# Two attention layers and two FFNs on one core: another order of the preparations in the first units, a wider spacing of stages in the FFN, other PSUM banks at its end and in the tail

## What is computed

```python
x = x + L0_xattn(ln(x), ctx)     # 32 query heads, 8 key/value heads of 128, rotary embedding, mask per batch
x = x + L0_ffn(ln(x))            # 512 -> 2 x 1376, silu(gate) * up, -> 512; weights are 4-bit with scale and zero per group
x = x + L1_xattn(ln(x), ctx)     # the same sizes, rms norm of q and k in place of rotary, one mask
x = x + L1_ffn(ln(x))            # router over 128 slots, top 8, softmax, gate from an uncertainty score; adds to ln(x)
```

## Time and profile before

| | PE | DVE | ACT | POOL |
|---|---|---|---|---|
| busy, us of 2639.3 | 2511.0 | 1813.5 | 1179.0 | 1063.3 |
| share | 95% | 69% | 45% | 40% |
| busy in 50 to 92 us | 27.77 | 37.37 | 25.19 | 21.48 |
| busy in 92 to 177 us | 67.77 | 57.02 | 41.39 | 38.38 |

### The profile page before, as it was taken

One profiled execution on the slowest core, in us unless ns is written; L12 is line 12 of the kernel. 1 busy time (PEld: TensorE's weight loads), 2 busy tenths in 40 slices (PEclk: granted clock), 3 DMA queues, 4 the chain that ended last, 5 costly groups with the idle time before them and its releaser, 6 DMA issues. The chain is left out here.

```text
span 2639.3 us, 45860 instructions
## 1 busy us (share of the span) xinstructions
PE 2511.0 (95%) x18307; PEld 1391.1 (53%) x18339; DVE 1813.5 (69%) x3271; ACT 1179.0 (45%) x2281; POOL 1063.3 (40%) x844
## 2 busy tenths in 40 slices
PE   7789999999999999999999889999999999999997
PEld 3355555555555554443444456665655655555543
DVE  7687887878777888643444556677776767765665
ACT  4555454545454544322222354444444444544333
POOL 3445444555544555222221243333334333334332
PEclk8899999999999999999999989999999999999999
DMA  6000000101000000101100100001010101000001
GB/s 193 17 25 17 33 25 25 33 9 33 9 33 17 12 7 25 41 25 32 34 16 15 36 17 1 1 33 40 10 33 9 33 9 33 25 15 1 1 1 64
DMA packets 57254, 68.73 MB, mean 26 GB/s; under 512 B 9858, under 2 KB 32966, under 8 KB 57040
## 3 DMA queue, kind: packets, MB, share of 16 engines
q1 hardware_dynamic: 57044, 65.79, 7.9%
HBM read 61.59 MB, written 4.19 MB: 25 GB/s over the span
## 5 line engine op out<-in xcount | busy, mean ns | idle before, releaser
L729 PE MATMUL PB<-WB,AR 128*128 128x512 f16 x3072 | 700.4, 382 | 25.8 <-issue 9.8
L685 PE MATMUL PB<-XTB,WB 128*128 128x512 f16 x3072 | 690.9, 383 | 3.4 <-DVE XTB L1634 3.4
L685 PEld LDWEIGHTS PB<-XTB,WB 128*128 128x128 f16 x3072 | 300.6, 99 | 352.9 <-issue 17.7
L729 PEld LDWEIGHTS PB<-WB,AR 128*128 128x128 f16 x3072 | 295.5, 98 | 359.3 <-issue 29.7
L1798 DVE SCALAR_TENSOR_TENSOR X<-PB,SML,X 128x512 f32<-128x512 f32 x256 | 191.6, 750 | 207.6 <-PE PB L729 201.1
L2312 POOL TENSOR_TENSOR AR<-AR,SML 128x512 f32<-128x512 f32 x128 | 144.7, 1152 | 327.1 <-DVE SML L1768 327.1
L1264 ACT ACTIVATE AR<-PB 128x512 f16<-128x512 f32 x256 | 132.2, 600 | 233.8 <-PE PB L768 233.8
L845 PE MATMUL PB<-XTB,AR 128*128 128x512 f16 (+1 forms) x864 | 199.5, 389 | 0.0
L1702 DVE TENSOR_TENSOR AR<-PB,AR 128x512 f16<-128x512 f32 x128 | 87.7, 688 | 159.4 <-ACT AR L1234 159.0
L2306 POOL TENSOR_TENSOR AR<-AR 128x512 f32<-128x512 f32 x128 | 185.8, 1451 | 24.5 <-DVE AR L1668 16.0
L2332 POOL TENSOR_TENSOR SML<-SML 128x16 f32<-128x16 f32 x32 | 98.1, 3065 | 239.3 <-DVE SML L1710 239.3
(11 more groups left out here) (222 smaller groups left out, 4010.6 us busy)
## 6 DMA issues: line engine op xcount, KB each, us to landing
STG<-in_wo SPq DMA_DIRECT2D x14, 1024.0 KB
STG<-in_wq SPq DMA_DIRECT2D x13, 1024.0 KB
STG<-in_qw_gu SPq DMA_DIRECT2D x40, 128.0 KB
STG<-in_ctxT SPq DMA_DIRECT2D x4, 1024.0 KB
X<-in_x SPq DMA_DIRECT2D x4, 1024.0 KB, 10.8
out_x<-X SPq DMA_DIRECT2D x16, 256.0 KB, 2.4
STG<-in_wk SPq DMA_DIRECT2D x14, 256.0 KB
STG<-in_wv SPq DMA_DIRECT2D x14, 256.0 KB
```

The costliest lines, as they stand in the source:

```text
L685: m = pe.do.matmul(b[:, :], wq[x][:, k, h * 128:(h + 1) * 128], XT[y][c][:, k, :], start=n == 0, stop=n == 11)
L729: m = pe.do.matmul(b[:, :], AT[x][:, h, t * 128:(t + 1) * 128], wo[y][:, h, :], start=n == 0, stop=n == 11)
```

## The change

No arithmetic is changed but the way that one low half is made. Five parts:

1. **First three units.** `w(0, 0, 2)` leaves `BY_POOL`: DVE makes its low half, and ACT's second pass and POOL's four subtractions are gone. The layer norm of chunk 1 comes earlier in unit 0: turned behind queries 2 and 3 in place of behind query 3 and between two empty output slots. In unit 2 the `scale` of context chunk 2 moves from slot 1 to slot 2. Ahead of the units, `w(0, 1, 1)` is prepared earlier, the mask and `w(0, 1, 0)` later.
2. **FFN.** For the three weights of layer 1's first head, `amax`, `peak`, `scale` and the two `low` move from slots (c=2, 2), (2, 3), (3, 0), (3, 2), (3, 3) of their slice to (2, 3), (3, 1), (3, 2), (3, 3) and slot 0 of the next slice. `peak` and `scale` of `w(1, 1, 0)` move one slot on.
3. **Last slice.** `down` uses banks 6, 7, 2, 3 for its four tiles.
4. **Start of layer 1.** Keys and values of unit 1 run ahead of the scores of unit 0, around `turn_k(0)`. Chunk 1's layer norm comes later in unit 0, and `w(1, 1, 2)` gets its `peak` in slot 8 and the rest in unit 1.
5. **Tail.** The normalised tiles of chunks 0 and 1 are turned one slot later, in banks 2, 3, 1, 6; `t_q` moves from slot 7 to slot 8; `TB_LG` and `TB_W` use bank 6 in place of 2.

```diff
-        BY_POOL = {("w", 0, 0, 2), ("w", 1, 0, 0), ("w", 1, 0, 1), ("w", 1, 0, 2), ("w", 1, 1, 0), ("w", 1, 1, 1), ("w", 1, 1, 2)}
+        BY_POOL = {("w", 1, 0, 0), ("w", 1, 0, 1), ("w", 1, 0, 2), ("w", 1, 1, 0), ("w", 1, 1, 1), ("w", 1, 1, 2)}
...
+        for slot, *stage in ((1, "ln_stats"), (2, "ln_norm", 0), (3, "ln_turn", 0), (3, "ln_norm", 1), (4, "ln_low", 0),
+                             (4, "ln_turn", 1), (5, "ln_low", 1)):
+            plan(0, 0, slot, stage[0], 0, 1, *stage[1:])
         plan_at(0, ("c", 1), (0, 0), (0, 1, 2), (0, 2, 3), (0, 3), (0, 4))
-        plan(0, 0, 1, "ln_stats", 0, 1)
-        plan_ln(0, 0, 0, 1, False)
...
-        plan_at(0, ("c", 2), (1, 9), (2, 0, 6), (2, 1, 7), (2, 4), (2, 7))
+        plan_at(0, ("c", 2), (1, 9), (2, 0, 6), (2, 2, 7), (2, 4), (2, 7))
...
-        plan_ln(1, 0, 2, 1, False)
-        plan(1, 0, 0, "peak", w(1, 1, 2), 6)
-        plan(1, 0, 1, "scale", w(1, 1, 2), 7)
+        for slot, *stage in ((1, "ln_norm", 0), (4, "ln_turn", 0), (5, "ln_low", 0), (5, "ln_norm", 1), (7, "ln_turn", 1),
+                             (8, "ln_low", 1)):
+            plan(1, 0, slot, stage[0], 2, 1, stage[1])
+        plan(1, 0, 8, "peak", w(1, 1, 2), 3)
+        plan(1, 1, 0, "scale", w(1, 1, 2), 7)
...
-                (u - 1, 9, ("t_stats", c)), (u, 1, ("t_norm", c, 0)), (u, 2, ("t_turn", c, 0)), (u, 3, ("t_norm", c, 1)),
-                (u, 5, ("t_turn", c, 1)), (u, 7, ("t_q", c)), (u + 1, 1, ("t_up", c)), (u + 1, 1, ("t_rq", c)),
+                (u - 1, 9, ("t_stats", c)), (u, 1, ("t_norm", c, 0)), (u, 3, ("t_turn", c, 0)), (u, 4, ("t_norm", c, 1)),
+                (u, 6, ("t_turn", c, 1)), (u, 8, ("t_q", c)), (u + 1, 1, ("t_up", c)), (u + 1, 1, ("t_rq", c)),
...
-        TB_TURN = {0: (2, 3, 0, 1), 1: (2, 3, 0, 1), 2: (6, 7, 6, 7), 3: (6, 7, 1, 3)}
+        TB_TURN = {0: (2, 3, 1, 6), 1: (2, 3, 1, 6), 2: (6, 7, 6, 7), 3: (6, 7, 1, 3)}
...
-        TB_R, TB_A, TB_LG, TB_W = (2, 2, 7, 7), (3, 3, 1, 1), (2, 2, 4, 2), (2, 2, 4, 4)
+        TB_R, TB_A, TB_LG, TB_W = (2, 2, 7, 7), (3, 3, 1, 1), (6, 6, 4, 2), (6, 2, 4, 4)
...
-            plan_prep_f(w(1, 0, s - 1), (s, 2, 2), (s, 2, 3), (s, 3, 0), (s, 3, 2), (s, 3, 3))
+            plan_prep_f(w(1, 0, s - 1), (s, 2, 3), (s, 3, 1), (s, 3, 2), (s, 3, 3), (s + 1, 0, 0))
...
-        plan_prep_f(w(1, 1, 0), (5, 0, 3), (5, 1, 0), (5, 1, 1), (5, 1, 3), (5, 2, 0))
+        plan_prep_f(w(1, 1, 0), (5, 0, 3), (5, 1, 1), (5, 1, 2), (5, 1, 3), (5, 2, 0))
...
+        def down_bank(s, t):
+
+            return 6 + t % 2 if s < 5 or t < 2 else t
...
-                else:
+                elif u > 1:
                     keys_values(u, 0)
                     keys_values(u, 1)
...
             for h in range(4):
                 queries(1, 0, h)
+            keys_values(1, 0)
             turn_k(0)
+            keys_values(1, 1)
             norm_q(0)
```

More of the change, by code:

```diff
@@ L349, in plan_at @@
                 plan(L, u, slot, *stage, *bank)
+        for slot, *stage in ((1, "ln_stats"), (2, "ln_norm", 0), (3, "ln_turn", 0), (3, "ln_norm", 1), (4, "ln_low", 0),
+                             (4, "ln_turn", 1), (5, "ln_low", 1)):
+            plan(0, 0, slot, stage[0], 0, 1, *stage[1:])
         plan_at(0, ("c", 1), (0, 0), (0, 1, 2), (0, 2, 3), (0, 3), (0, 4))
-        plan(0, 0, 1, "ln_stats", 0, 1)
-        plan_ln(0, 0, 0, 1, False)
         plan_at(0, w(0, 0, 2), (0, 9), (1, 0, 6), (1, 1, 7), (1, 2), (1, 3))
+        plan_ln(0, 2, 0, 2)
+        plan_at(0, ("c", 2), (1, 9), (2, 0, 6), (2, 2, 7), (2, 4), (2, 7))
         plan_at(0, w(0, 1, 2), (1, 5), (1, 7, 6), (1, 8, 7), (2, 0), (2, 1))
-        plan_ln(0, 2, 0, 2)
-        plan_at(0, ("c", 2), (1, 9), (2, 0, 6), (2, 1, 7), (2, 4), (2, 7))
         plan_prep(0, 3, ("c", 3))
@@ L379, in build @@
             plan(0, 30, hi, "unpack_hi", 0, k)
-        plan_ln(1, 0, 2, 1, False)
-        plan(1, 0, 0, "peak", w(1, 1, 2), 6)
-        plan(1, 0, 1, "scale", w(1, 1, 2), 7)
+        for slot, *stage in ((1, "ln_norm", 0), (4, "ln_turn", 0), (5, "ln_low", 0), (5, "ln_norm", 1), (7, "ln_turn", 1),
[3 more added lines that the diff above has]
+        plan(1, 1, 0, "scale", w(1, 1, 2), 7)
         for half in range(2):
-            plan(1, 0, 2 + half, "low", w(1, 1, 2), half)
+            plan(1, 1, 1 + half, "low", w(1, 1, 2), half)
         plan_ln(1, 2, 2, 2)
@@ L857, in down @@
                 for t in t01:
-                    b = bank(6 + t % 2, (x_add, ("f", s, c, t)))
+                    b = bank(down_bank(s, t), (x_add, ("f", s, c, t)))
                     e, last = 0, 3 * len(tiles) - 1
@@ L1078, in tensor @@
             ln_turn(0, 0, 1)
+            peak(w(0, 1, 1), 4)
             keep_warm(10, 0)
+            scale(w(0, 1, 1), 4)
             queries(0, 0, 0)
-            peak(w(0, 1, 1), 4)
             peak(w(0, 1, 0), 5)
             queries(0, 0, 1)
-            scale(w(0, 1, 1), 4)
             scale(w(0, 1, 0), 5)
@@ L1281, in ln_turn @@
                     if i == 0 and c == 3:
-                        act.wait_ge(w_lop, (w(0, 0, 2), 3))
+                        act.wait_ge(w_lo, (w(0, 0, 2), 3))
                     if i > 0:
@@ L1521, in scalar @@
             high(w(0, 0, 0))
+            high(w(0, 1, 1))
             turned_q(0, 0)
             turned_q(0, 1)
-            high(w(0, 1, 1))
             turned_q(0, 2)
@@ L1528, in scalar @@
             queries_0(0, 1)
+            high(w(0, 1, 0))
             queries_0(0, 2)
-            high(w(0, 1, 0))
             queries_0(0, 3)
@@ L1908, in down @@
                     dve.wait_ge(*added[c, t])
-                    dve.do.scalar_tensor_tensor(xs, PB[6 + t % 2][:, :], CY[:, :], xs, ALU.mult, ALU.add
+                    dve.do.scalar_tensor_tensor(xs, PB[down_bank(s, t)][:, :], CY[:, :], xs, ALU.mult, ALU.add
                                                 ).then_inc(x_add.of(("f", s, c, t)), 1)
@@ L2213, in vector @@
             ln_low(0, 0, 0)
+            largest(w(0, 1, 1))
+            peak(w(0, 1, 1), 4)
             low(w(0, 0, 0), 0)
             low(w(0, 0, 0), 1)
+            scale(w(0, 1, 1), 4)
             ln_low(0, 0, 1)
             keys_0(0)
-            largest(w(0, 1, 1))
             largest(w(0, 1, 0))
-            peak(w(0, 1, 1), 4)
             peak(w(0, 1, 0), 5)
             turned_q(0, 0)
-            mask()
-            scale(w(0, 1, 1), 4)
-            scale(w(0, 1, 0), 5)
-            turned_q(0, 1)
             low(w(0, 1, 1), 0)
             low(w(0, 1, 1), 1)
+            turned_q(0, 1)
+            scale(w(0, 1, 0), 5)
+            mask()
             queries_0(0, 0)
@@ L2234, in vector @@
             low(w(0, 1, 0), 0)
+            queries_0(0, 3)
             low(w(0, 1, 0), 1)
             turned_k(1)
-            queries_0(0, 3)
             values_0(1)
```

## The result

| | before | changed kernel |
|---|---|---|
| median of the runs, us | 2646.20 (2643.47 to 2647.24) | 2616.61 (2615.51 to 2617.64) |
| profiled execution, us | 2641.13 | 2616.46 |
| its span, us | 2639.3 | 2614.7 |

The ratio is 0.989, with a 95% interval of 0.9873 to 0.9907: 29.6 us less in the median, 24.7 in the profiled executions. The two differ because the profiled execution of the kernel before, 2641.13, was faster than each of its four other runs, while the changed kernel's lies at its median. The prediction was 2613.0, range 2603 to 2630.

The account below looks back on a forecast made before the run. PE, busy 95% of the span, was taken as the bound. Terms of -14.5, -4.6, -2.4, -3.6 and -8.5 us sum to -33.6, giving a profile of 2607.5 and a median of 2613.0 us, range 2603 to 2630.

Parts of the forecast that it names:

- A, first output of unit 0: In unit 1: with the low half on DVE this output starts at 111.5 in place of 120.6; -11.5 us.
- A, unit 0: Turns of chunk 1 in unit 0 waited 6.3 us for ACT's norm; 0 gained, DVE being busy.
- A, unit 2: Unit 2: `scale` of `c2` one query further back, -6.0 us; +3 for new waits at output tiles.
- B: FFN slices 1 to 3: waits at `peak` and `scale` go, partly given back through loads; -4.6 us, bounds 0 and -7.3.
- C: Last FFN slice: a `peak` wait of 3.04 us and part of a 3.54 go; -2.4 us, bounds 0 and -5.5.
- D: Unit 0 of layer 1: `norm_q`'s 2.6 us is covered, the turn of unit 1's keys waits 5.0; -3.6 us.
- E: Tail: 9.7 us of waits covered, new ones at `weigh` and one turn; -8.5 us, bounds -6 and -10.
- DVE takes the time back: Rival, first units onward: every low half blocked and each add late on DVE; only -14, 2632.6 us; chance 0.13.
- The load chain: Rival, FFN: the low half ends 2.7 us later in slices 1 and 2; -26 in all, about 2620.5; chance 0.10.
- The first part does what it says: Rival denied this: unit 0's output waits for something else ready shortly before 120.6; -23, 2623.5 us; chance 0.07.
- Little is given back: Rival: givebacks of 3 (first units), 2.8 (FFN) and 5.0 us (layer 1's start) don't come; -42, 2604.5; chance 0.10.
- The clock in 92 to 177 us: Rival, units 1 to 3: more frequent waits keep PE's clock at 0.50; slower, 2680 us if all halved; chance 0.03.

Follow-up runs that it names:

- Experiment 1: Changed kernel with POOL making the low half of `w(0, 0, 2)` again, behind a second pass of ACT; median 2624.14 us.
- experiment 2: Changed kernel with the two low halves of `w(0, 0, 2)` one slot earlier on DVE, slots 1 and 2 of unit 1; median 2608.39 us.
- experiment 6: Changed kernel with the layer norm of chunk 1 in unit 0 planned as before the change; one time, 2615.37 us.
- experiment 12: Changed kernel with the preparations of `w(0, 1, 1)`, `w(0, 1, 0)` and the mask ahead of the units in their old order; median 2616.97 us.
- experiment 10: Changed kernel with the `scale` of context chunk 2 back in slot 1 of unit 2; one time, 2621.01 us.
- Experiment 3: Changed kernel with SP loading the 4-bit words of slices 3 and 4 ahead of the layer 1 weights that wait; median 2609.37 us.
- Experiment 5: Changed kernel with unit 1's keys and values of layer 1 behind the scores of unit 0 again; median 2617.24 us.
- experiments 7: Changed kernel with the low halves of `w(0, 1, 2)` in slots 2 and 3 of unit 2 in place of 0 and 1; one time, 2617.66 us.

## Why the prediction came out as it did

The time lay 3.6 us above the forecast and inside the range; the change of the profile was forecast as -33.6 and was -24.7. That the median came so near is in part luck: the forecast was made on the profiled execution of before, 5.1 us below the median of its runs, and the changed kernel's profile shows 9.0 us more than the 2607.5 forecast for it. By the prediction's own sign ("wrong it is if the shift by unit 4 is under 10"), its largest part was wrong: the shift there is 6.7. By its own steps:

**A, first output of unit 0: right mechanism, wrong size.** Predicted -11.5, measured -4.4 (from the scores of unit 1, 0.3 late, to those of unit 2, 4.1 early). Three terms of one sum failed. "DVE may begin when the first pass has ended, at 105.7": the pass ended at 106.04 and DVE began at 107.92, because the instruction ahead of it waited for ACT (1.9 us). "I take 5.8 us for all of it": 107.92 to 115.87 are 7.95 (2.15 us), the low halves being 6.4 of it, near the upper bound of 7.0 that the prediction itself gave. "The clock behind a short wait should not fall, -2.4": the wait was still 4.85 and the output took 10.88, not 7.93 (3.0 us). With 0.1 at the hand-over they are the 7.1 that this output missed. The clock's part is the least certain: in nine other profiles with a wait of 4.8 the output took 9.32 to 9.62, once 10.88, so it fell every time, by 1.4 to 3.0 us, and the step gained 4.4 to 5.9. Experiment 1 shows that the low half was what held the output, experiment 2 that the order on DVE held the low half: with the pair one slot earlier, wait and lower clock are both gone, which is the state that the prediction had assumed.

**A, unit 0: right in this profile.** 0 predicted, 0.3 measured; most other profiles come 2 to 4 us later, with the lower clock of the first queries, which the prediction did not consider. The 6.3 at the turns became 2.5 there and 3.5 more at `weigh`. The reason given, a busy DVE, holds in the main; experiment 6 puts the early norm at 1.5, and experiment 12 the order ahead of the units at nothing.

**A, unit 2: right in sum, wrong in its parts.** -6.0 and +3 were predicted, -2.7 measured. The 3.9 of wait in the -6.0 does not follow from the rows: a query of 2.75 further back leaves 3.2 of the 5.9, and no term covers these. The new waits are larger than the 0.7 to 0.9 assumed (0.5, 2.1 and 2.4), and experiment 10 shows that the new slot, to which the whole -6.0 was put down, gives 1.2 by itself.

**B: right**, in sum and slice by slice. The chain of low half, load and words was read rightly: 8.15 us from low half to first use, 8.1 before; new wait 2.71, forecast 2.8. Experiment 3 takes the chain away and gains 7.2. The -1.3 of slice 2 has a fall of the clock in it (a `down` at 4.03); six other profiles, where it took 2.76, gain about 3 there, so the agreement in that slice is in part luck. **C and D: right**, -7.2 for -6.0, with the 5.0 at the turn of unit 1's keys and the 3.54 that moves to the keys (3.56). In C the norm of chunk 0 came later than forecast (2.6 of wait at its turn for 1.15, +1.4 for +0.8), while the 1.5 at `down` did not come. Experiment 5 shows that the keys' new place, which D counted as part of its gain, is worth nothing. How much the two more banks give is open.

**E: 2.7 too much.** The old waits all went and the two at `weigh` came (0.73 each, 0.8 forecast). The term that failed is the list of new waits: it lacked the query behind the turned mixture weights in bank 6, 2.64 us and in this profile 1.4 of clock. In eight of nine other profiles of this tail the clock did not fall there, and E is -7.6 by unit 29 rather than -6.3.

**Rivals.** "DVE takes the time back" is true in part: DVE ends the new waits of unit 0 (5.5 at `weigh`) and unit 2 (2.8 and 2.1), and in unit 1 it is an order on DVE and not its load. The low half was slowed by POOL as that rival said; with the pairs one slot earlier it cost no wait. The load chain did not come out worse than forecast. The first part does what it says. "Little is given back" did not come true; its sum is also off, since without the 3, the 2.8 and the 5.0 it is -44.4 and not -42, which would lie below the range. The clock in 92 to 177 us rose from 0.90 to 0.96, and in 50 to 92 us it stayed 0.76. Before, 92 to 177 us, then the changed kernel:

```profile
92.00:177.00 85.00, 67.77 (x478) 36.66 (x477) 57.02 (x100) 41.39 (x70) 38.38 (x30) 0.90 0.04 13
...
50.00:92.00 42.00, 26.17 (x196) 14.46 (x196) 34.52 (x55) 22.70 (x40) 21.38 (x17) 0.76 0.08 26
92.00:177.00 85.00, 73.54 (x593) 41.31 (x592) 70.00 (x116) 42.98 (x73) 35.84 (x27) 0.96 0.06 20
```

## What to carry to other kernels

When work moves to another engine, its start is set by that engine's own queue: look at what the instruction ahead of it waits for, not only at when its inputs are ready. Here one slot earlier, in the engine's idle time, was worth as much (8.2 us in the median) as the move itself (7.5). A queue of loads is an order as well: a load that must wait for memory holds back the ones behind it, and putting those first gained 7.2 us at no cost. And an edit that ends one wait should be priced with the next thing behind it: the next wait took back 1.6 of 2.6 us for the mixture weights, and for `w(0, 1, 2)` it was longer (5.6) than the two that it replaced (2.1 and 2.8). Last, before 2 us of a single profile are put down to an edit, the same rows should be read in other profiles of the same code: experiments 7 and 10 look different once the first output's clock, 1.5 us, is taken out.
